# VectorE turns u by blocks of 32 in the loop's pairs, the narrow products change banks, and A's first row tile has a transfer of its own

## The chip, the cores and the metric

One NeuronCore of a Trainium2 chip runs the whole kernel. The metric is the time of one execution on the device in microseconds, lower is better. Engines are named PE or TensorE (matmul), PEld (its weight loads), DVE or VectorE, ACT or ScalarE, POOL or GpSimd, SP or SyncE (here it only issues transfers).

## The reference

An adapter layer feeds a second one, and the input is added at the end. x has 2048 tokens of width 1024, everything in fp32.

```
c   = x @ W.T + 2 * (top-2 gates of 8 experts, biased by language) applied to low-rank x @ A.T, times B
z   = c @ Wf.T + bf                      (the second layer's base)
out = x + z + 2 * softmax(c @ Wrf.T) applied to low-rank c @ Af.T, times Bm
```

The gated low-rank activations of the first layer are called u (128 wide: 8 experts of rank 16), those of the second v (32 wide: 4 experts of rank 8).

## The kernel before, in words

The kernel first folds the two dense layers into one matrix (W times the second layer's weights, with seven products in place of eight, a Strassen-Winograd scheme), then applies it to the tokens. Every fp32 product is three matmuls: each operand is rounded to a short format ("high", by ScalarE) and the rest is taken by a subtraction ("low", by VectorE); the matmuls are high*high, high*low, low*high.

**Preparation** (about the first 106 us). 28 steps, `split_step(n)` on VectorE and `round_step(n)` on ScalarE, prepare a chunk of two blocks in a ring of six; TensorE multiplies it. `make_s1_t1` to `make_t4` on VectorE make the sums of blocks that later steps read, one instruction for each of four chunks (`HALF = 4`). The parts arrive by transfers that SP issues in a row. The very first chunk of A comes in two transfers, columns 256 to 511 (the row tiles 0 and 1, `row_tile(0)` and `row_tile(1)`) and then 0 to 255; its part of B comes on ScalarE's queue. TensorE keeps busy on constants (7 matmuls) until the first operands are there.

**The pairs** (16 tiles of 128 tokens, two at a time: 8 pairs). Pair 0 and pair 1 are written out (`first`, `second`), pairs 2 to 7 are "steady" and form a loop; on VectorE and ScalarE the last pair stands behind the loop, on TensorE it does not. For a pair, TensorE has in this order:

- seven narrow products (244 columns, 12 matmuls each) for gates and tails, in the order 1, 6, 2, 7, 5, 4, 3, in the banks `BANK_NA`, `BANK_NB`, `BANK_NC`; `narrow_products(j)` begins with a wait until the tails of the pair before are read (`tails_out`), since BANK_NA and BANK_NB are 4 and 5, and the tails lie in 4 and 5 (`BANK_T`);
- wide products 1, 6 and 2 (354 columns, 12 matmuls each), then `turn_u`, two 128x128 transposes of u into PSUM (L1508);
- wide product 7, `small_y` (u times the second layer's small columns: it waits for `ut_low_ready`), `lora(BANK_A)`, product 5, `lora(BANK_D)`, product 4, `mixed_tails` (waits for `vt_ready`), `lora(BANK_B)`, three `mixed`, product 3, `lora(BANK_C)`, `mixed(BANK_C)`.

VectorE adds the wide products into `rows` and the narrow ones into `narrow`, computes the gates and u (L1112 to L1145), adds u2 (L1153), splits the turned u into `ut_low` (L1160) after ScalarE made `ut_high` (L709), then does the softmax of the second layer, makes v and turns it with four block transposes (L1213), and splits the next pair's x (`split_x`) and block sums (`split_s`, made by `next_s`). The order of every engine is written out by hand; engines meet by semaphores that count up once a pair.

SP runs `load_pair(j + 2)`, which waits for `x_split` of each tile before it loads into the same buffer `stage`, and then `store(j)`, which waits for the adds into `rows`.

Of the kernel before, what the change touches and what calls it, by code (L numbers as in the profile page):

```python
# [5 lines left out]
def adaln_ffn_kernel(nc, part_2, part_1, part_3, part_4, tokens, gate_proj, mix_rows, language, out):  # L6
# [20 lines left out]
    P = 128  # L27
# [3 lines left out]
    HALF = KC // 2  # L31
# [51 lines left out]
    BANK_NA, BANK_NB, BANK_NC = 4, 5, 6  # L83
# [6 lines left out]
    with ctx:  # L90
# [138 lines left out]
        here_2_first = [sem(f"here_2_first_{i}") for i in range(3)]  # L229
# [95 lines left out]
        u_turned = sem("u_turned")  # L325
        ut_high_ready = sem("ut_high_ready")
# [192 lines left out]
        def scalar_program(act):  # L519
# [11 lines left out]
            copy(a_high[:, 0, 2 * P:ROWS_A], a12[:, 0, 2 * P:ROWS_A]).then_inc(first_high, 1)  # L531
# [143 lines left out]
            def pair(j, first=False, second=False, last=False):  # L675
# [37 lines left out]
                if steady and not last:  # L713
                    act.wait_ge(p2_done, j + 1)
                    round_x(j + 1, 0)
# [46 lines left out]
        def vector_program(dve):  # L762
# [8 lines left out]
            def minus(dst, a, b):  # L771
# [5 lines left out]
            low_part(a_low[:, 0, 2 * P:ROWS_A], a12[:, 0, 2 * P:ROWS_A], a_high[:, 0, 2 * P:ROWS_A])\  # L777
                .then_inc(first_low, 1)
            dve.wait_ge(first_b_high, 1)
            low_part(b_low[:, 0, 0:CUT[1]], b21[:, 0, 0:CUT[1]], b_high[:, 0, 0:CUT[1]]).then_inc(first_low, 1)  # L780
            dve.wait_ge(first_high, 2)
            low_part(a_low[:, 0, 0:2 * P], a12[:, 0, 0:2 * P], a_high[:, 0, 0:2 * P]).then_inc(first_low, 1)
            dve.wait_ge(first_high, 3)
            low_part(b_low[:, 0, CUT[1]:HB], b21[:, 0, CUT[1]:HB], b_high[:, 0, CUT[1]:HB]).then_inc(first_low, 1)
            dve.wait_ge(first_high, 4)
# [30 lines left out]
            def make_s4(k):  # L816
                dve.wait_ge(f_s2, k + 1)
                minus(s4[:, k, :], a12[:, k, :], s2[:, k, :]).then_inc(f_s4, 1)

            def make_t2(k):  # L820

                dve.wait_ge(here_4[k], 16)
                dve.wait_ge(f_t1, k + 1)
                minus(t2[:, k, :], b22[:, k, :], t1[:, k, :]).then_inc(f_t2, 1)

            def make_s3(k):

                dve.wait_ge(f_s1, k + 1)
                minus(s3[:, k, :], a11[:, k, :], a21[:, k, :]).then_inc(f_s3, 1)

            def make_t3(k):

                dve.wait_ge(here_4[k], 16)
                dve.wait_ge(f_t1, k + 1)
                minus(t3[:, k, :], b22[:, k, :], b12[:, k, :]).then_inc(f_t3, 1)

            def make_t4(k):
                dve.wait_ge(f_t2, k + 1)
                minus(t4[:, k, :], b21[:, k, :], t2[:, k, :]).then_inc(f_t4, 1)
# [87 lines left out]
            for k in range(1, HALF):  # L927
                make_s4(k)
# [11 lines left out]
            make_t2(2)  # L940
            make_t2(3)
            split_step(13)
            for k in range(HALF):
                make_s3(k)
# [17 lines left out]
            for k in range(HALF):  # L962
                make_t3(k)
# [15 lines left out]
            for k in range(HALF):  # L979
                make_t4(k)  # L980
# [70 lines left out]

            def pair(j, first=False, second=False, last=False):
                steady = not first and not second
                base = STEPS * j + VEC_START
# [93 lines left out]

                if not first:
                    dve.wait_ge(stored[0], 16 * j)  # L1150
                dve.wait_ge(r1_read, j + 1)
                dve.wait_ge(p6_done, j + 1)
                add_sums(rows[:, 0, wide_at(1)], bank(BANK_B), rows[:, 1, wide_at(0)]).then_inc(u2_read, 1)  # L1153
# [5 lines left out]
                dve.wait_ge(ut_high_ready, j + 1)  # L1159
                low_part(ut_low[:, :, :], ut_psum, ut_high[:, :, :]).then_inc(ut_low_ready, 1)  # L1160
                if first:
                    split_t(T4, C11)
                if second:
                    split_tn(T2)

                    make_tn(C11, C21, C11, t4n_made)
                    next_s(S1)
                    next_s(S2)
                    next_s(S3)

# [13 lines left out]
                if steady:  # L1184
                    add_u3()
# [10 lines left out]
                if second:  # L1196
                    next_s(S4)
# [18 lines left out]
                if steady:  # L1216
                    add_r22()
# [13 lines left out]
                if steady and not last:  # L1231
                    split_s(j + 1, S3)

# [17 lines left out]
                add_sums(rows[:, 1, wide_at(0)], bank(BANK_B), rows[:, 1, wide_at(0)]).then_inc(b_out, 1)  # L1251
                if not last:
# [14 lines left out]
        def tensor_program(pe):  # L1267
# [46 lines left out]
            for dt in range(2):  # L1314
                rows_product(0, dt, 0, HH)
# [321 lines left out]
```

## Time and profile before

| | |
|---|---|
| median of 3 runs | 324.57 us (324.01 to 324.74) |
| profiled execution | 324.45 us |
| its span, first to last instruction | 323.1 us |
| PE busy | 319.5 us, 99% of the span |
| DVE busy | 245.1 us, 76% |
| ACT busy | 127.9 us, 40% |
| transfers | 27.55 MB, mean 85 GB/s |
| granted TensorE clock | 1.000 |

The 1.35 us between the span and the execution's time lie before the first and behind the last instruction. Busy time is a sum over the span; a timeline gives for each instruction its start, its duration and, in brackets, how long its engine had stood idle and for whom. Consecutive instructions of an engine overlap a little in such rows, so the distance between two starts is what one costs.

### The profile page before, as it was taken

Reading aid. Unit: us, or ns where it says so; the run is one execution under the profiler, and the core shown is the slowest. Engines: PE = TensorE matmul, PEld = TensorE weight load, DVE = VectorE, ACT = ScalarE, POOL = GpSimd, SP = SyncE. Lnnn points to the kernel's source line nnn. Section 1 sums busy time; section 2 is a strip of 40 time slices with the busy share of each in tenths; the row PEclk is TensorE's granted clock in tenths of the full one; section 3 lists DMA queues with packets and bytes.
Section 4 is the critical chain, followed back from the end, with each engine's and each line's share of the span. In section 5 each row is a group of like instructions: output and inputs, shape, how many; then the busy total and the mean of one; then the engine's idle time right before and its main releaser. Section 6 shows DMA issues by size and latency. Waiting matters only on the chain.

```text
span 323.1 us, 5951 instructions
## 1 busy us (share of the span) xinstructions
PE 319.5 (99%) x2255; PEld 313.4 (97%) x2255; DVE 245.1 (76%) x540; ACT 127.9 (40%) x253; POOL 1.4 (0%) x11
## 2 busy tenths in 40 slices
PE   8999999999999999999999999999999999999996
PEld 5999999999999899899999999999999999999996
DVE  3999999998799778988866856757585595665543
ACT  3882846495147236225413503411430340342111
POOL 1000000000000000000000000000000000000000
PEclk9999999999999999999999999999999999999999
DMA  7999000000000311700330250060042015003003
GB/s 261 416 408 284 9 2 0 2 0 2 0 2 0 132 30 40 262 0 0 115 149 0 73 187 0 14 245 0 0 144 116 0 65 195 0 0 130 0 0 130
DMA packets 10702, 27.55 MB, mean 85 GB/s; under 512 B 3166, under 2 KB 4702, under 8 KB 10688
## 3 DMA queue, kind: packets, MB, share of 16 engines
q1 hardware_dynamic: 10256, 26.83, 23.5%
q10 hardware_dynamic: 432, 0.53, 0.5%
q8 instruction: 9, 0.15, 0.2%
q14 instruction: 5, 0.04, 0.0%
HBM read 18.97 MB, written 8.39 MB: 85 GB/s over the span
## 4 chain that ended last, share of the span: by engine, by line
PE 98%; DMA 1%; DVE 0%; issue 0%
PE sums L1269 97%; DMA in<-part 1%; PE sums L1508 1%; DVE rows L1047 0%; DVE b_high L775 0%
## 5 line engine op out<-in xcount | busy, mean ns | idle before, releaser
L1269 PE MATMUL sums<-b_high,a_high 128*128 128x256 f32 (+1 forms) x224 | 45.9, 289 | 0.2 <-DVE b_high L775 0.2
L1269 PE MATMUL sums<-b_low,a_high 128*128 128x256 f32 (+1 forms) x224 | 45.5, 287 | 0.0
L1269 PE MATMUL sums<-b_high,a_low 128*128 128x256 f32 (+1 forms) x224 | 45.5, 286 | 0.0
L1269 PEld LDWEIGHTS sums<-b_high,a_high 128*128 128x128 f32 x224 | 35.2, 191 | 1.1 <-ACT a_high L527 1.1
L1269 PEld LDWEIGHTS sums<-b_low,a_high 128*128 128x128 f32 x224 | 35.1, 191 | 0.0
L1269 PEld LDWEIGHTS sums<-b_high,a_low 128*128 128x128 f32 x224 | 34.9, 190 | 0.0
L1047 DVE TENSOR_TENSOR rows<-sums,rows 128x354 f32<-128x354 f32 x48 | 24.4, 522 | 9.7 <-PE sums L1269 9.3
L1047 DVE TENSOR_TENSOR narrow<-sums,narrow 128x244 f32<-128x244 f32 x30 | 12.4, 412 | 25.6 <-PE sums L1269 25.6
L1269 PE MATMUL sums<-t_high,s_high 128*128 128x354 f32 x96 | 31.6, 329 | 0.0
L1269 PE MATMUL sums<-t_low,s_high 128*128 128x354 f32 x96 | 31.1, 324 | 0.0
L1269 PE MATMUL sums<-t_high,s_low 128*128 128x354 f32 x96 | 31.1, 324 | 0.0
L1269 PE MATMUL sums<-ct_high,st_high 128*128 128x244 f32 (+1 forms) x80 | 25.6, 320 | 0.0
L1269 PE MATMUL sums<-ct_low,st_high 128*128 128x244 f32 (+1 forms) x80 | 25.5, 319 | 0.0
L1269 PE MATMUL sums<-ct_high,st_low 128*128 128x244 f32 (+1 forms) x80 | 25.5, 319 | 0.0
L693 ACT ACTIVATE pair_exp<-top 128x1 f32<-128x1 f32 x16 | 3.9, 287 | 48.1 <-DVE top_at L1120 48.0
L527 ACT ACTIVATE s_high<-s_plain 128x512 fp32r<-128x512 f32 x28 | 17.3, 626 | 13.1 <-PE sums L1269 12.4
L1269 PE MATMUL sums<-c_high,st_high 128*128 128x354 f32 x64 | 21.0, 328 | 0.0
L1269 PE MATMUL sums<-c_low,st_high 128*128 128x354 f32 x64 | 20.8, 325 | 0.0
L1269 PE MATMUL sums<-c_high,st_low 128*128 128x354 f32 x64 | 20.7, 324 | 0.0
L769 DVE TENSOR_TENSOR b_low<-in,b_high 128x530 fp32r<-128x530 f32 (+2 forms) x29 | 19.9, 687 | 0.0
L769 DVE TENSOR_TENSOR s_low<-s_plain,s_high 128x512 fp32r<-128x512 f32 x28 | 18.9, 685 | 0.0
L1269 PEld LDWEIGHTS sums<-t_low,s_high 128*128 128x128 f32 x96 | 18.2, 189 | 0.0
(149 smaller groups left out, 821.9 us busy)
## 6 DMA issues: line engine op xcount, KB each, us to landing
stage<-tokens SPq DMA_DIRECT2D x14, 512.0 KB, 4.1
out<-rows SPq DMA_DIRECT2D x14, 512.0 KB, 4.8
in<-part SPq DMA_DIRECT2D x7, 585.0 KB, 9.0
in<-part SPq DMA_DIRECT2D x4, 777.0 KB, 14.1
in<-part SPq DMA_DIRECT2D x4, 265.0 KB, 16.6
rows<-tokens SPq DMA_DIRECT2D x2, 512.0 KB, 14.1
out<-rows SPq DMA_DIRECT2D x3, 192.0 KB, 2.3
c_plain<-gate_proj SPq DMA_DIRECT2D x1, 544.0 KB, 18.3
```

Of the source, the lines that this page charges most:

```text
L527: return nc.scalar.activation(out_, in_, ACT.Copy)
L693: ins = nc.scalar.activation(pair_exp[:, t:t + 1], top[:, t, 0:1], ACT.Exp, bias=top[:, t, 1:2], scale=-1.0)
L769: return nc.vector.tensor_tensor(dst, src, as_f32(high), ALU.subtract)
L1047: return nc.vector.tensor_tensor(dst, n, onto, ALU.add)
L1269: return nc.tensor.matmul(out_, lhs, rhs, start=start, stop=stop, skip_group_check=True)
L1508: last = nc.tensor.transpose(ut_psum[:, t, :], u[:, t, :], ident[:, :])
```

## The change

Four things, of which the first is the largest.

1. **u is turned by VectorE in pairs 2 to 6.** 16 transposes of 32-row blocks write into the gate columns of `narrow`, which are free once u is made. After the first 8 a semaphore lets ScalarE round the first half, after 16 the second; VectorE splits each half. The turned u no longer goes through PSUM. TensorE's last pair stands behind the loop (`last=True`) and keeps its own transposes, as do pairs 0 and 1.
2. **TensorE's order in pairs 2 to 6.** Product 5 goes ahead of `small_y`; `lora(BANK_B)` and product 3 go ahead of `mixed_tails`. VectorE and ScalarE follow: the adds of u3 and r22 come right after the split of u, `next_s(S4)` behind the maximum of the second softmax, the splits of S2 and S3 later, ScalarE's rounding of x's first tile before that of u.
3. **Banks.** The narrow products use 6, 7 and 4 in place of 4, 5 and 6; the wait for `tails_out` moves from before narrow product 1 to before narrow product 5, and ScalarE waits for `tails_out` before its first narrow copy.
4. **The start.** A's row tiles 0 and 1 come in two transfers and are rounded, split and multiplied in two pieces. The sums S3, T3, T4 are made in one instruction each in place of four, S4 in two, T2 in three.

```diff
-    BANK_NA, BANK_NB, BANK_NC = 4, 5, 6
+    BANK_NA, BANK_NB, BANK_NC = 6, 7, 4
...
+        def ut_plain_at(partitions, c, n):
+            h, c = divmod(c, P // 2)
+            return narrow[partitions, :, h, c:c + n]
+        def ut_plain_half(h):
+            return narrow[:, :, h, 0:P // 2]
+        def half_of(t, h):
+            return t[:, :, h * P // 2:(h + 1) * P // 2]
...
-            sp.dma_start(in_2[:, 0, 2 * P:ROWS_A], part_2[0, :, 2 * P:ROWS_A]).then_inc(here_2_first[0], 16)
+            sp.dma_start(in_2[:, 0, row_tile(0)], part_2[0, :, row_tile(0)]).then_inc(here_2_first[0], 16)
+            sp.dma_start(in_2[:, 0, row_tile(1)], part_2[0, :, row_tile(1)]).then_inc(here_2_first[3], 16)
...
                 if steady:
+                    act.wait_ge(tails_out, j)
                     act.wait_ge(p1n_done, j - 1)
...
+                if steady and not last:
+                    act.wait_ge(p2_done, j + 1)
+                    round_x(j + 1, 0)
+                if steady and not last:
+                    act.wait_ge(u_half_turned, j - 1)
+                    copy(half_of(ut_high, 0), ut_plain_half(0)).then_inc(ut_half_high, 1)
                 act.wait_ge(u_turned, j + 1)
-                copy(ut_high[:, :, :], ut_psum).then_inc(ut_high_ready, 1)
+                if steady and not last:
+                    copy(half_of(ut_high, 1), ut_plain_half(1)).then_inc(ut_high_ready, 1)
+                else:
+                    copy(ut_high[:, :, :], ut_psum).then_inc(ut_high_ready, 1)
...
-            for k in range(HALF):
-                make_s3(k)
+            make_s3()
...
+            def turn_u(j):
+                dve.wait_ge(u_ready, j + 1)
+                for h in range(2):
+                    for q in range(h * P // BLOCK // 2, (h + 1) * P // BLOCK // 2):
+                        rows_at = slice(q * BLOCK, (q + 1) * BLOCK)
+                        for i in range(P // BLOCK):
+                            at = slice(i * BLOCK, (i + 1) * BLOCK)
+                            ins = nc.vector.transpose(ut_plain_at(at, q * BLOCK, BLOCK), u[rows_at, :, at])
+                    ins.then_inc((u_half_turned, u_turned)[h], 1)
...
-                if steady:
-                    next_s(S4)
-                    if not last:
-                        split_s(j + 1, S2)
+                if turning:
+                    turn_u(j)
+                    dve.wait_ge(ut_half_high, j - 1)
+                    low_part(half_of(ut_low, 0), ut_plain_half(0), half_of(ut_high, 0))
                 dve.wait_ge(ut_high_ready, j + 1)
+                if turning:
+                    low_part(half_of(ut_low, 1), ut_plain_half(1), half_of(ut_high, 1)).then_inc(ut_low_ready, 1)
...
+                if turning:
+                    add_u3()
+                    add_r22()
...
+                if turning:
+                    split_s(j + 1, S2)
...
+                if turning:
+                    split_s(j + 1, S3)
                 if not last:
                     split_x(j + 1, 1)
...
             def narrow_products(j):
-                pe.wait_ge(tails_out, j)
...
+                pe.wait_ge(tails_out, j)
                 pe.wait_ge(s_split, 4 * j + S_NO[S1])
                 narrow_of_s(BANK_NC, S1, tn_high[T1], tn_low[T1], True).then_inc(p5n_done, 1)
...
-                if steady:
+                if last:
                     turn_u()
...
                 of_s(BANK_B, S3, t_high[T3], t_low[T3], False).then_inc(p7_done, 1)
+                if turning:
+                    product_5(j)
                 if steady:
                     small_y()
                 lora(BANK_A, 0, 0)
...
+                if turning:
+                    lora(BANK_B, 1, 0)
+                    product_3(j)
+                    mixed_tails(j)
...
-            with pe_loop(2, PAIRS) as j:
+            with pe_loop(2, PAIRS - 1) as j:
                 pair(j)
+            pair(PAIRS - 1, last=True)
```

## Rows read from the trace of the kernel before

**Rows 1.** Waits of TensorE: line, releaser: total us, times, longest.
```profile
PE sums L1269 <- PEq L1630: 0.8, 1, 0.8
PE sums L1269 <- DVE b_high L775: 0.2, 1, 0.2
```
**Rows 2.** The chain that ended last (start, us), then busy time in one pair.
```profile
226.67 0.22 PE sums L1508 x2
226.89 27.10 PE sums L1269 x192
...
211.10:238.40 27.30, 27.30 (x196) 27.28 (x195) 18.39 (x51) 8.18 (x20) 0.00 (x0) 1.00 0.22 77
```
**Rows 3.** Timeline of VectorE and ScalarE in pair 4: start, duration.
```profile
225.08 0.52 DVE L1047 TENSOR_TENSOR rows<-sums,rows 128x354 f32<-128x354 f32 x1
...
227.21 1.05 ACT L527 ACTIVATE st_high<-stage 128x1024 fp32r<-128x1024 f32 x1
...
231.88 0.97 DVE L1213 STREAM_TRANSPOSE vt_plain<-v 32x64 f32<-32x64 f32 x4
...
233.77 0.41 DVE L769 TENSOR_TENSOR vt<-vt_plain,vt 32x256 fp32r<-32x256 f32 x1 [0.35 <-ACT vt L527]
```
**Rows 4.** Timeline of TensorE, starts of turn_u, small_y, mixed_tails, narrow products 7 and 3.
```profile
226.51 0.38 PE L1508 MATMUL sums<-ident,u 128*128 128x128 f32 x2
...
228.68 0.32 PE L1269 MATMUL sums<-c_high,ut_high 128*128 128x352 f32 x1
...
234.55 0.46 PE L1269 MATMUL sums<-mix,vt 98*128 98x316 f32 x2
...
242.51 0.39 PE L1269 MATMUL sums<-t_narrow,s_high 128*128 128x244 f32 x2
...
246.62 0.27 PE L1269 MATMUL sums<-ct_high,s_high 128*128 128x244 f32 x1
```
**Rows 5.** Timeline of VectorE behind mixed_tails and into pair 5.
```profile
235.36 0.68 DVE L769 TENSOR_TENSOR s_low<-s_plain,s_high 128x512 fp32r<-128x512 f32 x1
235.96 0.81 DVE L1047 TENSOR_TENSOR rows<-sums,narrow 128x632 f32<-128x632 f32 x1
236.69 0.95 DVE L1047 TENSOR_TENSOR rows<-sums,rows 128x354 f32<-128x354 f32 x2
237.55 1.21 DVE L769 TENSOR_TENSOR st_low<-stage,st_high 128x1024 fp32r<-128x1024 f32 x1
238.69 0.52 DVE L1047 TENSOR_TENSOR rows<-sums,rows 128x354 f32<-128x354 f32 x1
239.15 0.69 DVE L769 TENSOR_TENSOR s_low<-s_plain,s_high 128x512 fp32r<-128x512 f32 x1
241.43 0.41 DVE L1047 TENSOR_TENSOR narrow<-sums,narrow 128x244 f32<-128x244 f32 x1 [1.58 <-PE sums L1269]
...
244.41 0.68 DVE L877 TENSOR_TENSOR s_plain<-stage 128x512 f32<-128x512 f32 x1
```
**Rows 6.** Loads of x into stage, 225 to 262 us: issues (start of first and last), landing.
```profile
L451 SPq DMA_DIRECT2D stage<-tokens x2: 354/354/355, 235.7 to 238.9; - x2
...
DMA to landing us min/median/max: 3.5/3.7/4.0
```
**Rows 7.** Timeline of the start; last, window 3 to 4 us, DMA share before the GB/s.
```profile
3.72 0.29 DVE L775 CAST b_high<-in 128x256 fp32r<-128x256 f32 x1 [1.92 <-DMA in<-part]
...
4.13 0.50 PEld L1269 LDWEIGHTS sums<-b_high,a_high 128*128 128x128 f32 x2 [1.10 <-ACT a_high L527]
...
4.92 0.29 ACT L527 ACTIVATE bt_high<-in 128x128 fp32r<-128x128 f32 x1
...
7.83 0.64 ACT L527 ACTIVATE a_high<-in 128x512 fp32r<-128x512 f32 x1 [2.62 <-DMA in<-part]
...
8.76 1.16 PE L1269 MATMUL sums<-b_high,a_high 128*128 128x256 f32 x8
...
3.00:4.00 1.00, 0.93 (x3) 0.03 (x1) 0.28 (x2) 0.42 (x1) 0.00 (x0) 1.00 1.10 393
```
**Rows 8.** DMA queues of the page: packets, MB, share of 16 engines' span.
```profile
q8 instruction: 9, 0.15, 0.2%
```

More of the change, by code:

```diff
@@ L228, in adaln_ffn_kernel @@
         here_4 = [sem(f"here_4_{k}") for k in range(HALF)]
-        here_2_first = [sem(f"here_2_first_{i}") for i in range(3)]
+        here_2_first = [sem(f"here_2_first_{i}") for i in range(4)]
         gate_here = sem("gate_here")
@@ L814, in make_s2, with make_s4, make_t2, make_s3 @@
                 minus(s2[:, k, :], s1[:, k, :], a11[:, k, :]).then_inc(f_s2, 1)
[L816 to L839, printed above, removed]
+            def make_s4(k, n=1):
+                dve.wait_ge(f_s2, k + n)
+                minus(s4[:, k:k + n, :], a12[:, k:k + n, :], s2[:, k:k + n, :]).then_inc(f_s4, n)
+            def make_t2(k, n=1):
+                for i in range(k, k + n):
+                    dve.wait_ge(here_4[i], 16)
+                dve.wait_ge(f_t1, k + n)
+                minus(t2[:, k:k + n, :], b22[:, k:k + n, :], t1[:, k:k + n, :]).then_inc(f_t2, n)
+            def make_s3():
+                dve.wait_ge(f_s1, HALF)
+                minus(s3, a11, a21).then_inc(f_s3, HALF)
+            def make_t3():
+                dve.wait_ge(f_t1, HALF)
+                minus(t3, b22, b12).then_inc(f_t3, HALF)
+            def make_t4():
+                dve.wait_ge(f_t2, HALF)
+                minus(t4, b21, t2).then_inc(f_t4, HALF)
             def add_out(q, c, lower, onto):
@@ L926, in vector_program @@
             make_s2(3)
-            for k in range(1, HALF):
-                make_s4(k)
+            make_s4(1, 3)
             make_t2(0)
@@ L961, in vector_program @@
             split_step(15)
-            for k in range(HALF):
-                make_t3(k)
+            make_t3()
             dve.wait_ge(lang_here, 16)
@@ L978, in vector_program @@
             split_step(16)
-            for k in range(HALF):
-                make_t4(k)
+            make_t4()
             for n in range(17, 20):
@@ L1050, in vector_program @@
             BLOCK = 32
+            def turn_u(j):
[7 more added lines that the diff above has]
+                    ins.then_inc((u_half_turned, u_turned)[h], 1)
             def pair(j, first=False, second=False, last=False):
                 steady = not first and not second
+                turning = steady and not last
                 base = STEPS * j + VEC_START
@@ L1195, in pair @@
                                         negate=True).then_inc(neg_max_ready, 1)
-                if second:
+                if second or turning:
                     next_s(S4)
@@ L1313, in tensor_program @@
             pe.wait_ge(first_b_high, 1)
-            for dt in range(2):
-                rows_product(0, dt, 0, HH)
+            rows_product(0, 0, 0, HH)
             pe.wait_ge(first_low, 1)
-            for dt in range(2):
-                rows_product(0, dt, 0, LH)
+            rows_product(0, 0, 0, LH)
+            pe.wait_ge(first_high, 2)
+            rows_product(0, 1, 0, HH)
             pe.wait_ge(first_low, 2)
@@ L1463, in narrow_products, with product_3, pair @@
                 narrow_of_s(BANK_NC, S4, cn_high[B22], cn_low[B22], False).then_inc(p3n_done, 1)
-            def pair(j, first=False, second=False):
+            def product_3(j):
+                pe.wait_ge(s_split, 4 * j + 4)
+                pe.wait_ge(r22_read, j + 1)
+                of_s(BANK_C, S4, cw_high[B22], cw_low[B22], False).then_inc(p3_done, 1)
+            def pair(j, first=False, second=False, last=False):
                 steady = not first and not second
+                turning = steady and not last
                 s_no = S_NO_FIRST if first else S_NO
@@ L1523, in pair @@
                 of_x(BANK_A, 0, 1, cw_high[B21], cw_low[B21], False).then_inc(p2_done, 1)
-                if steady:
+                if last:
                     turn_u()
-                else:
+                if not steady:
                     small_y()
@@ L1536, in pair @@
                 lora(BANK_A, 0, 0)
+                if second or last:
+                    product_5(j)
                 if not first:
-                    product_5(j)
                     pe.wait_ge(d_out, j)
@@ L1545, in pair @@
                 of_x(BANK_B, 1, 1, t_high[T4], t_low[T4], False).then_inc(p4_done, 1)
-                if not steady:
+                if turning:
+                    lora(BANK_B, 1, 0)
+                    product_3(j)
+                    mixed_tails(j)
+                elif last:
+                    mixed_tails(j)
+                    lora(BANK_B, 1, 0)
+                else:
                     lora(BANK_B, 1, 0)
                     mixed_tails(j)
-                else:
-                    mixed_tails(j)
-                    lora(BANK_B, 1, 0)
                 mixed(BANK_A, 0, 0).then_inc(a_done, 1)
```

65 lines of the change are left out of this document (33 added, 32 removed).

## The prediction

> **What bounds the kernel now.** I read four views, in this order. The first is the list of waits, to see whether TensorE ever stands still: it waits twice, 0.8 us for its sequencer and 0.2 us for VectorE's first rounding, both before 4.2 us [rows 1]. The second is the chain that ended last, to see what fills the rest: it is TensorE alone, in the loop 27.10 us of matmuls and 0.22 us for the two transposes of u, pair after pair [rows 2]. So the kernel is one stream of matmuls. Work taken out of that stream is time won, work taken off any other engine is worth nothing, and any wait put into the stream costs its whole length. The third view is the timeline of one pair by engine, for how early each semaphore comes before TensorE asks for it. The fourth is the first 10 us, where the stream depends on transfers.
>
> **What leaves the stream.** In the pairs 2 to 6 TensorE no longer transposes u: 5 x 0.22 = 1.1 us less [rows 2]. Pair 7 keeps its transposes. All other matmuls stay, in another order. At this size a page of the Trainium skill can be weighed. The row says 0.22 us for two fp32 transposes. The page "VectorE: DVE Perf Modes", section "The three transpose paths", gives 390 ns for one 128x128 transpose on TensorE (bf16); by it 5 x 2 x 0.39 = 3.9 us would go, an estimate from that page, and the time would be 320.6. The trace has a duration for this very operation, so the row decides.
>
> **What VectorE gets.** 16 block transposes a pair, each of 32x64 elements, the shape it already turns v in: four of those take 0.97 us at 0.232 us each, so one begins 0.246 us after the other [rows 3]. Sixteen take 15 x 0.246 + 0.232 = 3.92 us. Their partitions differ from v's (the output moves over four groups of 32, with v the input does), and no row shows that form. Bounds: from below 0.14 us apart, if they overlapped by the 0.09 us that other VectorE instructions do (0.52 us long and 0.43 apart) [rows 5]; from above 0.30 apart, if each were as long as a 128x128 instruction on ScalarE, 0.29 [rows 7]. I take 0.246, the same shape. VectorE is not the bound: it works 18.4 us in the 27.3 of a pair [rows 2], so there is room for the sum; what matters is two places where its result is due.
>
> *Place one, before small_y.* Times in the clock of rows 3 to 6, with the change written into that pair. The add of u2 starts at 225.08 as now [rows 3], the transposes at 225.52, their end is 229.44. The first half is rounded and split under the second. ScalarE's rounding of x, 1.05 us [rows 3], now stands ahead of it but begins when product 2 is done, near 226.8, and ends before 227.9. The second half: ScalarE 229.48 to 229.77 (0.29), VectorE to 230.08 (0.29, from the same bound). TensorE reaches small_y at 228.68 [rows 4] - 0.22 + 1.95 for product 5, now ahead of it (product 7 is as long: 228.68 - 226.51 - 0.22) = 230.41. At the start the first weight load comes 0.12 us after VectorE's end (4.01 to 4.13) [rows 7], and a load takes 0.11 of its own, since two transposes with a load each pass in 0.22; so the semaphore is due at 230.41 - 0.23 = 230.18. **It is 0.10 early.** Cost 0; if that cover is gone each 0.1 us is 0.5 us in all.
>
> *Place two, before narrow product 7 of the next pair.* Product 3 and lora(BANK_B) now stand before mixed_tails, which starts at 234.55 - 0.22 + 0.49 + 1.95 = 236.77 [rows 4], 2.22 us later. Behind it VectorE has the tails add (0.73 to the next start), two adds (0.86), the split of S3 that was moved here (0.60), the split of x's second tile (1.14), the add of c (0.46), the split of S1 (0.60), the narrow u2 add (0.41) [rows 5]: 4.80 us from 237.26, so 242.06. Narrow product 7 starts at 242.51 - 0.22 = 242.29 [rows 4], so its semaphore is due at 242.06. **It is exactly in time**: 0 to 0.1 us a pair. I take 0, and keep 5 x 0.1 = 0.5 us for the range.
>
> **Other edits of the loop.** vt is ready at 234.18 for mixed_tails at 234.55 [rows 3, 4]. Its chain begins with small_y, 1.73 us later, and mixed_tails is 2.22 later: more room than now. The new banks let narrow products 1, 6, 2 and 7 start before the tails are read; TensorE doesn't wait there today [rows 1], so nothing is won. ScalarE's and TensorE's moved waits on the tails end at 238.07 (237.26 + 0.81), when narrow product 1 still runs: it is three products of 1.37 us before product 7 [rows 4] and ends at 239.55. SP is moved too: the load of x's second tile waits for the split of x, now done at 240.66 instead of 238.76. It lands 3.5 to 4.0 us after its issue, some 0.14 us behind the split [rows 6], at 244.3 to 244.8, and the sum S1 that is due at 244.41 - 0.22 = 244.19 [rows 5] waits 0.1 to 0.6 us. The add queued behind it, r22n, is needed for narrow product 3 at 246.62 - 0.22 [rows 4]; at the latest it starts 0.61 behind S1, at 245.4, and with 0.41 is done at 245.8, due at 246.17, 0.35 us early. The stores, queued behind that load on SP, wait for the add of c, over at 241.1; the next add of u2, which waits for them, is at 225.08 + 27.1 = 252.2, 11 us later, and a load of the same 512 KB takes 4.0 at most. Cost 0.
>
> **The start.** Now A's first tile is 64 KB in its own transfer, and every later transfer on SP is issued some 0.45 us later. The first weight load, at 4.13, follows the rounding of b (3.72 to 4.01) [rows 7], which is not A's, so A's half size brings little. Whatever it brings ends at the next chunk: its a is rounded from 7.83 to 8.47, and the matmuls that read it start at 8.76 without a gap [rows 7], due 0.23 earlier at 8.53. A gain is capped at 0.06 us. A loss: if issue set the landings, chunk 1 lands 0.45 late and costs 0.4. But from 3 us on the DMA engines are full (share 1.10) [rows 7], so their rate sets it and the late issue is hidden. The smaller rows make more packets; I take 0.05 lost, range -0.06 to +0.4. The merged make_s3, make_s4, make_t2, make_t3 and make_t4 do in one instruction what up to four did, 0.6 us apart [rows 5]; their first chunk comes up to 1.8 us later and their last no later. TensorE has no wait in all this stretch [rows 1], but how much room it had I leave open: 0 as long as VectorE runs three chunks ahead.
>
> **The peeled last pair.** TensorE now leaves a loop once. No row shows it leaving one. From below 0, the way straight code runs; from above one fetch of instructions: 9 packets took 0.2% of 16 engines' 323.1 us, 1.15 us each [rows 8]. I take 0, since pairs 0 and 1 run as straight code without a wait [rows 1].
>
> **Sum.** The profiled execution took 324.45 us, 323.1 of it span. 324.45 - 1.1 + 0.05 = 323.4. The median of the runs is 324.57, 0.12 above it, so 323.5.
>
> **Rivals.**
> (a) *The stream closes up, as summed*: 323.5; its own range 323.2 to 323.8. For it: both places close at measured durations. Chance 0.57.
> (b) *Waits of 0.1 to 0.2 us a pair take the transposes' place*, at narrow product 7 above all, or chunk 1 lands late at the start: 0.5 to 1.0 us given back, 324.0 to 324.5, no measurable change. For it: the margin of 0.00 and of 0.10. Against: both use start-to-start times of the same instructions. Chance 0.25.
> (c) *The slower side: the block transposes are dearer than v's.* At distance d the wait at small_y is 15 x (d - 0.246) - 0.10 a pair, five times; it eats the gain from d = 0.267 and makes the kernel slower by 0.2% from d = 0.275. At the upper bound 0.30 it is 0.7 us a pair, 3.5 in all: 327.0. Against: v's transposes too change their partitions from one to the next, and all take 0.232 us. Chance 0.10. The skill's page "VectorE: DVE Perf Modes" says in "Rules for kernel authors" that a 128x128 transpose belongs on TensorE when PSUM may take it; by that rule this rival is the one to expect. In the trace TensorE is the full engine and VectorE has a third of its time free, which speaks the other way.
> (d) *Leaving the loop costs a fetch*, once: 323.5 + 1.15 = 324.65, no change. Chance 0.08. The skill's "Runtime: NRT & Kernel Launch", section "Instruction fetch mechanics", says that a taken branch out of the fetched window stalls; the loop's branch back costs nothing in [rows 1], and the way out is not taken but fallen through.
>
> **How the numbers follow.** A measurement here tells about 0.2%, 0.65 us, from no change: faster means under 323.92, slower over 325.22. (a) is faster; of (b) a fifth is; (c) is half slower, half same; (d) is the same, with a third of it slower by a longer fetch. Faster 0.57 + 0.05 = 0.62; slower 0.05 + 0.03 = 0.08, and 0.02 more for two rivals at once, 0.10; same the rest, 0.28. The range goes from the fast end of (a), with the 0.3 us by which a median of runs moves, 322.9, to the upper end of (b), 324.6; above lie (c) and part of (d).
>
> **What would show it.** In the profile after: 10 fewer transposes of L1508's kind but 80 more block transposes; chain of the loop 27.10 us per pair with no 0.22 piece; TensorE's waits still below about 1 us in all. Right at place one: the ut_low split ends 0.1 us before small_y could start. Wrong in (b): a wait of TensorE on `narrow` (narrow product 7) or on b or a of chunk 1. Wrong in (c): mean of a block transpose over 0.25 us, a wait on ut_low five times. Wrong in (d): one wait of TensorE near 293 us that no engine releases.

## The result and the profile after

The changed kernel takes 324.84 us (median of 20 executions, 323.99 to 327.97), the kernel before beside it 324.46 (20, 323.94 to 325.24). The ratio over all executions is 1.003, interval 1.0016 to 1.0044: slower by 0.3%. The forecast was 323.5 and faster. The executions of the changed kernel lie in two groups, 12 at 323.99 to 325.0 and 8 at 325.91 to 327.97, with nothing between; the kernel before has no second group. The profiled execution, at 323.99, is the shortest of the first group. So its profile shows the milder case.

The page of the changed kernel first: span, then busy time, share and instructions of each engine.

```profile
span 322.7 us, 6000 instructions
...
PE 318.1 (99%) x2245; PEld 311.8 (97%) x2245; DVE 263.2 (82%) x614; ACT 128.5 (40%) x259; POOL 1.4 (0%) x11
```

TensorE is busy 1.4 us less than the 319.5 of before, VectorE 18.1 us more. Of the 1.4 the forecast has 1.1, the transposes taken out. The next view, the waits of TensorE, answers to [rows 1] and shows what came in (PEq and SPq are the parts of TensorE and SyncE that issue their work).

```profile
PE sums L1313 <- DVE a_low L796: 0.9, 1, 0.9
PE sums L1313 <- PEq L1690: 0.8, 1, 0.8
```

The 0.2 us for b_high is gone, and in its place stands 0.9 us for a_low. The chain that ended last says where:

```profile
1.21 0.42 SPq L445
...
1.67 3.41 DMA in<-part
...
5.11 0.42 ACT a_high L543
...
5.55 0.43 DVE a_low L796
...
6.03 110.52 PE sums L1313 x846
...
143.29 164.57 PE sums L1313 x1164
307.86 0.22 PE sums L1562 x2
```

Two things are to be read. From 143.29 on the loop is one piece of 164.57 us with no 0.22 in it: pairs 2 to 6 no longer turn u, and no listed wait stands in their place. In the kernel before the same stretch (from behind the transposes of pair 1 to those of pair 7) lasts 165.66, so the loop gained 1.09 us; the forecast was 1.1. And TensorE's unbroken stream now begins at 6.03, behind a transfer, where it began at 4.13 [rows 7]. The timeline of the start, same columns as [rows 7]:

```profile
1.67 0.43 SPq L446 DMA_DIRECT2D in<-part  x1
...
3.12 0.31 ACT L543 ACTIVATE a_high<-in 128x128 fp32r<-128x128 f32 x1 [0.15 <-DMA in<-part]
3.32 0.29 DVE L802 CAST b_high<-in 128x256 fp32r<-128x256 f32 x1 [1.52 <-DMA in<-part]
...
3.76 0.51 PE L1313 MATMUL sums<-b_high,a_high 128*128 128x256 f32 x1
...
4.06 0.31 ACT L543 ACTIVATE a_high<-in 128x128 fp32r<-128x128 f32 x1 [0.63 <-DMA in<-part]
...
5.11 0.42 ACT L543 ACTIVATE a_high<-in 128x256 fp32r<-128x256 f32 x1 [0.73 <-DMA in<-part]
...
5.55 0.42 DVE L796 TENSOR_TENSOR a_low<-in,a_high 128x256 fp32r<-128x256 f32 x1 [0.86 <-ACT a_high L543]
...
6.03 0.50 PE L1313 MATMUL sums<-b_high,a_high 128*128 128x256 f32 x2 [0.87 <-DVE a_low L796]
...
8.08 0.63 ACT L543 ACTIVATE a_high<-in 128x512 fp32r<-128x512 f32 x1 [2.04 <-DMA in<-part]
```

The first matmul on real data comes earlier, at 3.76. But the transfer of A's columns 0 to 255 (L446) is now third on SP's queue. It goes out at 1.67, and its rounding starts at 5.11. TensorE is through with row tiles 0 and 1 at about 5.2 and stands until 6.03. Chunk 1 is late too, 8.08 against 7.83 [rows 7], but here TensorE doesn't wait for it: its matmuls start at 9.10, 0.34 us after the 8.76 of before, and that distance is already 0.36 at 6.37 (6.01 before). In this execution the first of pair 0's transposes comes at 116.56 instead of 116.22, a loss of 0.34 us. The rest of the 0.9 was won before and just behind the wait: 0.40 by the earlier beginning (3.76 for 4.16), since B's first part is rounded at 3.32 instead of 3.72 [rows 7], and 0.13 because the matmuls reach their full rate earlier. In the kernel before, two matmuls of 256 columns still took 0.43 us at 5.58; here two take 0.23 at 4.65.

The windows of the start, with DMA share and GB/s as the last two columns, answer to the last of [rows 7]:

```profile
3.00:4.00 1.00, 1.00 (x4) 0.30 (x3) 0.68 (x3) 0.31 (x1) 0.00 (x0) 1.00 0.92 287
4.00:5.00 1.00, 0.96 (x6) 0.72 (x6) 0.44 (x2) 0.31 (x1) 0.00 (x0) 1.00 0.93 255
```

The DMA engines show a busy share of 0.92 between 3 and 4 us where it was 1.10, and move 287 GB/s where they moved 393: the rate fell by more than the share.

The loop, pair 4, at the two places that the forecast watched:

```profile
225.48 3.99 DVE L1083 STREAM_TRANSPOSE narrow<-u 32x64 f32<-32x64 f32 x16
229.50 0.64 DVE L796 TENSOR_TENSOR ut_low<-narrow,ut_high 128x128 fp32r<-128x128 f32 x2
...
230.38 0.33 PE L1313 MATMUL sums<-c_high,ut_high 128*128 128x352 f32 x1
...
241.59 0.41 DVE L1070 TENSOR_TENSOR narrow<-sums,narrow 128x244 f32<-128x244 f32 x1
...
242.25 0.39 PE L1313 MATMUL sums<-t_narrow,s_high 128*128 128x244 f32 x2
...
245.16 0.69 DVE L905 TENSOR_TENSOR s_plain<-stage 128x512 f32<-128x512 f32 x1 [0.93 <-DMA stage<-tokens]
```

Sixteen block transposes take 3.99 us, 0.25 from start to start (3.92 forecast). ut_low is done at 230.14 (230.08), small_y starts at 230.38 (230.41). The narrow u2 add ends at 242.00 (242.06), narrow product 7 starts at 242.25 (242.29). TensorE waits at neither. The late load of x's second tile makes VectorE wait 0.93 us here, and next to nothing of it reaches TensorE. One pair earlier the wait is 1.04 us, and there some of it does, at the first matmul of narrow product 3 (`ct_high,s_high`):

```profile
218.08 0.69 DVE L905 TENSOR_TENSOR s_plain<-stage 128x512 f32<-128x512 f32 x1 [1.04 <-DMA stage<-tokens]
...
219.06 0.27 PE L1313 MATMUL sums<-t_narrow,st_low 128*128 128x244 f32 x1
219.24 0.35 PE L1313 MATMUL sums<-ct_high,s_high 128*128 128x244 f32 x1
219.43 0.27 PE L1313 MATMUL sums<-ct_low,s_high 128*128 128x244 f32 x1
```

The distances are 0.18 and 0.19 us where such matmuls otherwise start 0.11 apart, 0.15 us lost. The list of waits doesn't have it, since these rows overlap by 0.16 us (0.27 long, 0.11 apart) and a shorter delay leaves no gap.

### The profile page after: what moved, and what is told of

It reads as the page before. It is cut to its first block, busy times and chain, and to the rows that moved or that the text cites. A ratio compares the mean times of both kernels' runs of the same rounds, so it can differ in the third digit from the quotient of the medians.

```text
span 322.7 us, 6000 instructions
## 1 busy us (share of the span) xinstructions
PE 318.1 (99%) x2245; PEld 311.8 (97%) x2245; DVE 263.2 (82%) x614; ACT 128.5 (40%) x259; POOL 1.4 (0%) x11
## 4 chain that ended last, share of the span: by engine, by line
PE 97%; DMA 1%; DVE 0%; SPq 0%; ACT 0%; issue 0%
PE sums L1313 97%; DMA in<-part 1%; PE sums L1562 0%; DVE rows L1070 0%; DVE a_low L796 0%; ACT a_high L543 0%; SPq L445 0%; SPq L444 0%
## 5 line engine op out<-in xcount | busy, mean ns | idle before, releaser
L1083 DVE STREAM_TRANSPOSE narrow<-u 32x64 f32<-32x64 f32 x80 | 18.8, 235 | 1.1
```

The costliest lines, as they stand in the source:

```text
L1083: ins = nc.vector.transpose(ut_plain_at(at, q * BLOCK, BLOCK), u[rows_at, :, at])
```

## Experiments

Each kernel was timed beside the kernel before on the same chip: 324.23, 324.34 and 324.37 us in the three groups. "New loop" is everything of the change but the start.

### Which half costs: the whole again, the new loop alone, the new start alone

`e4_after_again` is the changed kernel once more.

> The changed kernel itself again, for its spread beside the other three on one chip and for a second profile. Both theories: ratio 1.002 to 1.005, executions from 324.0 to 328. Theory S: if the profiled execution is a slow one, its loop is again 27.09 us a pair and all of the loss lies before 12 us. Theory L: the loop's pairs are unequal.

`e1_old_start` puts back the start and keeps the rest:

```diff
-            sp.dma_start(in_2[:, 0, row_tile(0)], part_2[0, :, row_tile(0)]).then_inc(here_2_first[0], 16)
-            sp.dma_start(in_2[:, 0, row_tile(1)], part_2[0, :, row_tile(1)]).then_inc(here_2_first[3], 16)
+            sp.dma_start(in_2[:, 0, 2 * P:ROWS_A], part_2[0, :, 2 * P:ROWS_A]).then_inc(here_2_first[0], 16)
...
-            copy(a_high[:, 0, row_tile(0)], a12[:, 0, row_tile(0)]).then_inc(first_high, 1)
-            act.wait_ge(here_2_first[3], 16)
-            copy(a_high[:, 0, row_tile(1)], a12[:, 0, row_tile(1)]).then_inc(first_high, 1)
+            copy(a_high[:, 0, 2 * P:ROWS_A], a12[:, 0, 2 * P:ROWS_A]).then_inc(first_high, 1)
...
```

The splits on VectorE and the order of the first matmuls go back with it.

> The changed kernel with its start put back (A's row tiles 0 and 1 in one transfer, rounded, split and multiplied together as before); loop, banks and merged sums stay changed. Theory S (the start is what went wrong: in the profile after, A's columns 0 to 255 came third on SP's queue, TensorE waited 0.87 us for them at 5.1 us, and in some executions the clock falls as well): the time is 1.1 us below the kernel before, 323.4, ratio 0.996 to 0.998, mean clock 0.998 or more in nearly all executions, all within 1.5 us. Theory L (the slow executions come from the loop, where x's second load now lands at the time it is read): executions still spread over 3 to 4 us, a third of them above 325.8, ratio 1.000 to 1.003.

`e2_new_start_alone` is the kernel before with only that part of the diff put in, the other way round.

> The kernel before with the new start alone (two transfers for A's row tiles 0 and 1, two roundings, two splits, the new order of the first matmuls); loop, banks and sums as before. Theory S: 0.4 us later than before in a good execution (324.9), and in a third of the executions 1.5 to 3 us later, part of them with a mean clock of 0.993 to 0.995; ratio 1.003 to 1.006. Theory L: 0.4 us later throughout, ratio about 1.001, no execution above 325.8.

| | median us (range) | ratio to before |
|---|---|---|
| e4, all | 326.09 (324.64 to 326.65) | 1.0044 (1.0028 to 1.006) |
| e1, new loop | 323.36 (323.06 to 324.11) | 0.9968 (0.9956 to 0.998) |
| e2, new start | 326.41 (324.93 to 328.29) | 1.006 (1.0036 to 1.0085) |

The new loop gains 0.3% (0.87 us by the medians, 1.04 by the ratio), the new start costs 0.6%. e4 falls into the two groups again, 4 executions at 324.64 to 324.95 and 8 at 325.94 to 326.65. Its profiled execution, at 325.96, is one of the upper group, and its waits and windows show what happened in it. Columns of the windows as in [rows 7]: PE busy with its matmuls (x) first, and the granted clock before the DMA share.

```profile
PE sums L1313 <- DVE a_low L796: 1.4, 1, 1.4
...
7.00:8.00 1.00, 1.00 (x6) 1.00 (x6) 0.00 (x0) 0.00 (x0) 0.00 (x0) 0.50 1.05 351
8.00:9.00 1.00, 1.00 (x7) 1.00 (x6) 0.24 (x1) 0.24 (x1) 0.00 (x0) 0.50 0.94 365
9.00:10.00 1.00, 1.00 (x6) 1.00 (x6) 0.96 (x3) 0.59 (x2) 0.00 (x0) 0.50 1.00 407
```

TensorE waits 1.4 us until 6.47, and just behind that the granted clock is 0.50, the lower of its two levels (1.2 GHz), for three us: 6 or 7 matmuls in each instead of 10 or 11. Against the profiled execution of the first time the span is 1.9 us longer (324.6 to 322.7): the unbroken stream begins 0.44 us later (6.47 for 6.03), and its first piece, the same 846 matmuls, takes 112.06 us instead of 110.52, 1.54 by the clock. The loop's piece is 164.49 against 164.57, so nothing of this is lost in the loop. The window from 7 us on has 10 matmuls in e1:

```profile
7.00:8.00 1.00, 1.00 (x10) 1.00 (x9) 0.29 (x1) 0.29 (x1) 0.00 (x0) 1.00 0.93 356
```

The Trainium skill's page "TensorE: Matmul & The Clock Gate", section "What's actually happening", says that the lower clock is the default and that activity of the array releases the higher one. The rows agree: the fall of the clock stands behind the one long wait.

### The transfers or the pieces

The start changed two things, two transfers for one and two pieces of work for one. `e5_one_transfer_pieces` is the changed kernel with one transfer, the pieces kept:

```diff
-            sp.dma_start(in_2[:, 0, row_tile(0)], part_2[0, :, row_tile(0)]).then_inc(here_2_first[0], 16)
-            sp.dma_start(in_2[:, 0, row_tile(1)], part_2[0, :, row_tile(1)]).then_inc(here_2_first[3], 16)
+            sp.dma_start(in_2[:, 0, 2 * P:ROWS_A], part_2[0, :, 2 * P:ROWS_A]).then_inc(here_2_first[0], 16)
...
-            act.wait_ge(here_2_first[3], 16)
```

> The changed kernel with A's row tiles 0 and 1 again in one transfer of 128 KB; they are still rounded, split and multiplied in two pieces. Theory T (the additional transfer ahead of A's columns 0 to 255 and of every chunk on SP's queue is the whole loss): no wait of TensorE over 0.4 us before 10 us, ratio 0.996 to 0.998, as the kernel with the old start (0.9968). Theory P (the two pieces and their new order on VectorE and TensorE cost too): ratio above 0.999.

`e6_two_transfers_whole` is e1 with the two transfers of the change (their lines aren't shown), and one rounding behind both:

```diff
             act.wait_ge(here_2_first[0], 16)
+            act.wait_ge(here_2_first[3], 16)
             copy(a_high[:, 0, 2 * P:ROWS_A], a12[:, 0, 2 * P:ROWS_A]).then_inc(first_high, 1)
```

> The old start with the additional transfer alone: row tiles 0 and 1 come in two transfers, ScalarE waits for both and rounds them together; matmuls in the old order. Theory T: columns 0 to 255 land 0.9 us late, TensorE waits about 0.6 to 1.2 us for their split, ratio 1.002 to 1.007, a third or more of the executions above 325.6. Theory P: ratio 0.997 to 0.999, no execution above 325.

e5 measured 323.57 (323.31 to 323.91), ratio 0.9975 (0.9967 to 0.9984), in one group: the pieces cost nothing that can be told (e1 has 0.9968). e6 measured 326.21 (325.68 to 327.08), 1.0057 (1.0044 to 1.0069), 5 executions, but its trace shows a second cause, so that it decides nothing. Timeline of ScalarE, then a window:

```profile
3.98 1.28 ACT L543 ACT_TABLE_LOAD   x1 [3.98 <-DMA in<-part]
5.28 0.72 ACT L543 ACTIVATE a_high<-in 128x256 fp32r<-128x256 f32 x2
...
6.00:7.00 1.00, 1.00 (x5) 1.00 (x6) 1.00 (x4) 0.53 (x3) 0.00 (x0) 1.00 0.91 370
```

With two waits ahead of the first rounding, the load of ScalarE's table stood behind the first of them: 3.98 instead of 1.69. TensorE began at 5.75, behind a wait of 1.8 us, at 5 to 7 matmuls in a us until 11.9. The column of the clock says 1.00 there, because the trace has no record of the clock before 11.91 us; in the trace of the kernel before the first is at 6.04, where the matmuls become faster. So a low clock at the very start shows in the count of matmuls and not in that column. This could explain why 4 of the 8 long executions of the changed kernel, and all 5 of e2's, are listed with a mean clock of 1.000; none of them was profiled, so it isn't shown. `e9_two_transfers_one_wait` repeats the question with a single wait (against e1):

```diff
-            sp.dma_start(in_2[:, 0, 2 * P:ROWS_A], part_2[0, :, 2 * P:ROWS_A]).then_inc(here_2_first[0], 16)
+            sp.dma_start(in_2[:, 0, row_tile(0)], part_2[0, :, row_tile(0)]).then_inc(here_2_first[0], 16)
+            sp.dma_start(in_2[:, 0, row_tile(1)], part_2[0, :, row_tile(1)]).then_inc(here_2_first[0], 16)
...
-            act.wait_ge(here_2_first[0], 16)
+            act.wait_ge(here_2_first[0], 32)
```

> As e6_two_transfers_whole, but both transfers raise one semaphore and ScalarE waits for it once, so that its table load isn't held behind the first wait (in e6 it began at 3.98 us in place of 1.69). Theory T (the additional transfer alone is the loss): row tile 1 lands near 4.0 us, columns 0 to 255 near 5.0, TensorE starts at 4.6 to 4.8 and waits again before the second half; ratio 1.000 to 1.005 with a group of slow executions. If e6 was slow by its table load alone: ratio 0.996 to 0.998.

It measured 325.25 (324.13 to 326.99), 1.0024 (1.001 to 1.0038), where the same program with one transfer (e1) had 0.9968. Six of its 12 executions lie at 325.65 or above, five of these with a mean clock of 0.994 or 0.995. Its profiled one, at 326.99 us, waits for both parts of A and shows the fall:

```profile
PE sums L1310 <- DVE a_low L794: 1.1, 1, 1.1
...
PE sums L1310 <- ACT a_high L543: 0.5, 1, 0.5
...
7.00:8.00 1.00, 1.00 (x7) 1.00 (x7) 0.21 (x2) 0.00 (x0) 0.00 (x0) 0.50 0.98 365
```

So it is the second transfer, not the pieces (0.9 us of that one execution is lost in the loop, as shown below). Up to 6 us the changed kernel moved this,

```profile
DMA packets 856, 1.19 MB, mean 199 GB/s; under 512 B 89, under 2 KB 729, under 8 KB 856
```

and e1, with the same bytes to fetch, this:

```profile
DMA packets 765, 1.42 MB, mean 236 GB/s; under 512 B 78, under 2 KB 590, under 8 KB 765
```

That is 91 more packets and 0.23 MB less. Both the late issue of columns 0 to 255 (1.67 for 1.21) and the smaller packets can delay them; how the two share the delay was not taken apart.

### The place in the queue, and the clock by itself

`e7_columns_on_act` leaves both transfers and exchanges what comes next: A's columns 0 to 255 go second on ScalarE's queue, the rest of B's first chunk third on SP's.

```diff
-            sp.dma_start(in_2[:, 0, 0:2 * P], part_2[0, :, 0:2 * P]).then_inc(here_2[0], 16)
+            sp.dma_start(in_2[:, 0, ROWS_A + CUT[1]:IN_W], part_2[0, :, ROWS_A + CUT[1]:IN_W])\
+                .then_inc(here_2_first[2], 16)
...
-            act.dma_start(in_2[:, 0, ROWS_A + CUT[1]:IN_W], part_2[0, :, ROWS_A + CUT[1]:IN_W])\
-                .then_inc(here_2_first[2], 16)
+            act.dma_start(in_2[:, 0, 0:2 * P], part_2[0, :, 0:2 * P]).then_inc(here_2[0], 16)
```

> The changed kernel, with A's columns 0 to 255 as the second transfer on ScalarE's queue and the rest of B's first chunk (201 KB) as the third on SP's: the two swap queues. Theory T: columns 0 to 255 are there near 4.5 us, as before the change, the rest of B is needed 0.7 us after them; TensorE waits 0 to 0.4 us, ratio 0.996 to 0.999. If it is the number of transfers or the smaller rows that cost and not the place in the queue: as the changed kernel, 1.003 or more.

`e8_constants_in_the_gap` gives TensorE five matmuls on constants in the place of the wait, as it has them before its first operands. The late transfer stays late.

```diff
+            for _ in range(5):
+                mm(bank(BANK_WARM, 0, BANK), ones[:, 0:P], ones, start=True, stop=True)
             pe.wait_ge(first_low, 4)
             tiles_product(0, 1, 0)
```

> The changed kernel, and TensorE multiplies constants five times (512 columns, 1.07 us at the upper clock) into an unused bank where it waited for A's columns 0 to 255. Theory C (the wait has a second price: TensorE's idleness of 0.9 to 1.4 us in the first microseconds makes the clock fall to its lower level for some 3 us in part of the executions, 1.5 to 2 us each): the slow group disappears, all executions within 1 us around 324.0 to 324.7, ratio 0.998 to 1.001. If the slow group is only a later landing, it stays: executions above 325.8, ratio 1.003 or more.

e7: 324.18 (323.83 to 324.7), ratio 0.9997 (0.9988 to 1.0006). The wait of 0.9 us is now two of 0.2 us, and no execution is above 324.7. The place of the transfer was most of the loss, and the upper group goes with the wait. But e7 just misses its 0.996 to 0.999, and it is still 0.6 us above e5, timed beside it with one transfer; that part stays open.

e8: 324.75 (323.92 to 325.34), 1.0014 (1.0005 to 1.0022), also just outside what was expected. The upper group is gone here too. That doesn't give the price of the late data, since the constants outlast the wait. In the profiled execution A's split is done at 5.80, and TensorE takes 1.58 us for the five, part of them still at the lower rate:

```profile
5.34 1.93 PE L1313 MATMUL sums<-const-bfloat16-1.0 128*128 128x512 bf16 x5
6.92 0.59 PE L1313 MATMUL sums<-b_high,a_high 128*128 128x256 f32 x2
```

The two parts of the price are better read from the groups. The lower group of e4 has its median at 324.73, 1.4 us above e1's 323.36 beside it. The upper groups lie higher by another 1.6 us (e4) and 1.9 us (the first timing).

What sorts an execution into a group is not shown. The profiled ones with a second transfer give a hint: TensorE had reached its full rate at about 3.5 us in the two in which the clock fell (e4, with a wait of 1.4 us; e9, with 0.5 and 1.1), by 4.4 in the changed kernel's first (0.9 us, no fall) and near 5 us in e2 (1.1 us, no fall).

### The loop: what gains, and how near the two places are

`e12_order_without_turning` is e1 in which TensorE turns u in pairs 2 to 6 as before, while orders, banks and merged sums stay new:

```diff
-                if last:
+                if steady:
                     turn_u()
...
-                if turning:
-                    turn_u(j)
-                    dve.wait_ge(ut_half_high, j - 1)
-                    low_part(half_of(ut_low, 0), ut_plain_half(0), half_of(ut_high, 0))
```

> The version with the old start, with the new order, banks and merged sums, but u is turned by TensorE into PSUM in pairs 2 to 6 as before (and ScalarE and VectorE round and split it whole). Theory G (the gain of the loop is the transposes and nothing else): 1.1 us above e1_old_start, ratio 1.000, between 0.9993 and 1.001. If order, banks or merged sums gave part of the gain: below 0.999.

It measured 324.43 (324.1 to 324.93), ratio 1.0003 (0.9995 to 1.0012), and its chain is that of [rows 2] again:

```profile
226.31 0.22 PE sums L1544 x2
226.53 27.09 PE sums L1297 x192
```

By the medians it is 1.1 us above e1 (beside another group of runs). The whole gain of the loop is the ten transposes; the new order only makes room for VectorE's, and banks and merged sums cost nothing that can be told.

`e10_two_more_turns` and `e11_two_turns_before_narrow` are e1 with two more block transposes in each turn, into a tile that nobody reads: ahead of VectorE's turning of u (pairs 2 to 6), or ahead of the narrow u2 add (pairs 2 to 7).

```diff
+                    dve.wait_ge(u_ready, j + 1)
+                    for i in range(2):
+                        nc.vector.transpose(spare[0:BLOCK, :, i * BLOCK:(i + 1) * BLOCK], u[0:BLOCK, :, i * BLOCK:(i + 1) * BLOCK])
                     turn_u(j)
```

> The version with the old start (0.9968), and in pairs 2 to 6 VectorE makes two more block transposes, into a spare tile, ahead of the sixteen: 0.49 us more before the second half of u is split. Theory M (the margin before small_y is 0.10 us, as worked out in the prediction): TensorE waits 0.4 us in each of five pairs, 1.9 us in all, ratio 1.002 to 1.004. If the margin is larger than 0.5 us: ratio 0.997 as without them.

> The version with the old start (0.9968), and in pairs 2 to 7 VectorE makes two more block transposes, into a spare tile, ahead of the narrow add of u2: 0.49 us. Theory M (the margin before narrow product 7 is 0 to 0.05 us in pairs 3 to 7): TensorE waits 0.45 us in each of five pairs, 2.2 us in all, ratio 1.003 to 1.005. If the margin is larger than 0.5 us: ratio 0.997.

e10: 324.47 (323.99 to 324.89), 1.0 (0.9992 to 1.0009). e11: 325.07 (324.87 to 325.65), 1.0021 (1.0012 to 1.003). Both lose, but less than expected (1.002 to 1.004 and 1.003 to 1.005), since the two extra transposes took less time. Timeline of VectorE and TensorE in e10:

```profile
225.20 0.35 DVE L1203 STREAM_TRANSPOSE spare<-u 32x64 f32<-32x64 f32 x2
225.48 1.19 DVE L1080 STREAM_TRANSPOSE narrow<-u 32x64 f32<-32x64 f32 x5
...
229.98 0.32 PE L1313 MATMUL sums<-t_high,s_low 128*128 128x354 f32 x1
230.16 0.43 PE L1313 MATMUL sums<-c_high,ut_high 128*128 128x352 f32 x1
230.43 0.32 PE L1313 MATMUL sums<-c_low,ut_high 128*128 128x352 f32 x1
```

Two cost 0.28, 0.14 each; both read the same 32 partitions and write the same 32. The turning of u, which writes to others each time, stays at 0.24 to 0.25 (five in 1.19), and so do the four of v, which write to the same 32 partitions but read others each time (0.246 apart [rows 3]). The Trainium skill's page "VectorE: DVE Perf Modes", section "Two Vector instructions with no wait between them", says that an instruction whose input or output starts in another group of 32 partitions than the last one's is held until the earlier have finished; these rows agree.

The loop's piece of the chain is 165.53 in e10 and 165.47 in e11, against 164.50 in e3 below. The starts of TensorE's matmuls say where the 1.0 us goes. In e10 small_y (230.16) and its second matmul start 0.18 and 0.27 us behind the one before, where 0.16 is usual: 0.13 lost, and 0.12 to 0.15 in each of the five pairs. From 0.28 added, so place one has about 0.15 us of room, 0.10 by the forecast. The other 0.3 us of e10 is lost at narrow product 3, in three pairs. In e11 narrow product 7 loses 0.22 a pair in four pairs and 0.15 in the fifth, from 0.29 added. So place two has about 0.07 us; the forecast had 0.00. By the ratios e11 is 1.7 us above e1. Some 1.0 of it is the loop; in its profiled execution 0.2 more is a wait for chunk 1, which landed at 8.06; the rest stays open.

`e3_old_start_load_early` is e1 with `split_x(j + 1, 1)` ahead of `split_s(j + 1, S3)`, so that SP issues the load of x's second tile earlier.

```diff
-                if turning:
-                    split_s(j + 1, S3)
                 if not last:
                     split_x(j + 1, 1)
+                if turning:
+                    split_s(j + 1, S3)
```

> As e1_old_start, and VectorE splits x's second tile before S3 in pairs 2 to 6, so that SP can issue the load of x 0.6 us earlier. Theory S: the same as e1_old_start, 323.4. Theory L: fewer slow executions than e1_old_start, median at least 0.3 us lower.

323.55 (323.14 to 323.81), 0.9971 (0.9961 to 0.9982): by the times the same as e1. The profiled executions differ. The loop's piece in e1 and e3, then in e9, which has e1's loop:

```profile
142.78 165.06 PE sums L1309 x1164
...
143.22 164.50 PE sums L1309 x1164
...
145.52 76.27 PE sums L1310 x540
221.79 0.11 issue
221.90 88.94 PE sums L1310 x624
```

In e3 VectorE waits for that load only in pair 1, and from one small_y to the next TensorE takes 27.09 us from pair 2 to pair 6. In e1 it waits 0.97 to 1.07 us in pairs 2 to 5, and narrow product 3 of the next pair comes 0.1 to 0.2 us late each time, 0.6 us in all. In e9 the wait reaches 1.24 us and the loss is 0.9; in e4 and e6, with waits up to 0.9 us, there is none. So in the same code the late load costs TensorE 0 to 0.9 us an execution, and it costs where VectorE waits more than about 0.9 us. e1's profiled execution is its longest (324.11), and e3's lost 0.5 us at the start, to a wait for chunk 1, so that the medians don't show what the earlier load is worth.

## Why the prediction failed

**What bounds the kernel** held. One stream of matmuls; work taken out of it was won in full, and waits put into it were paid. What did not hold is that a wait costs its length: 0.9 us cost 0.34 against the profiled execution of before, since the beginning was earlier, and 1.4 us in e4 was followed by 1.5 us of lower clock.

**What leaves the stream** held: 1.1 forecast, 1.09 in the chain, 0.87 to 1.04 in e1's times, nothing without it (e12).

**VectorE's two places** held, to 0.06 us each, with no wait of TensorE; the room measured is about 0.15 us at the first and 0.07 at the second (0.10 and 0.00 forecast). Rival (b)'s waits of 0.1 to 0.2 us a pair did not come at these places, but at narrow product 3 they came, in one pair of the changed kernel's first profile and in four of e1's. Rival (c) did not: the transposes take 0.236 us in the mean, 0.25 apart. Rival (d) did not: no wait near 293 us.

**The other edits of the loop** held for the banks, the moved waits and the merged sums. The load of x's second tile was taken for free with 0.35 us to spare before narrow product 3; it lands up to 4.3 us after its issue instead of 4.0, S1 waits 0.85 to 1.04 us in pairs 2 to 5 where 0.1 to 0.6 was forecast, and the room is used up: 0.15 us lost in that profile, 0 to 0.9 us in others. That the loop's gain still came out at 1.09 in it is partly luck, since that execution had the loss in one pair only.

**The start is the step that failed**, the term "I take 0.05 lost, range -0.06 to +0.4". It followed the first transfer (little gained, where the first matmul in fact came 0.40 us earlier, since B's first part was there earlier) and chunk 1 (0.25 us late, inside the range) and passed over the transfer between them, A's columns 0 to 255, which went from second to third on SP's queue. Its reason, "the DMA engines are full, so their rate sets it and the late issue is hidden", took a busy share for a fixed rate: the share was 0.92 and the rate 287 GB/s instead of 393. Those columns were rounded at 5.11 instead of 4.28, TensorE waited 0.9 to 1.4 us, and 8 of 20 executions took about 1.9 us more. The two long ones of that kind that were profiled (in e4 and e9) spent it on the lower clock behind the wait; for the others the clock is argued, not shown. In the term's own units: measured is 324.84 - (324.46 - 1.10) = 1.5 us by the medians of the first timing, and 326.09 - 323.36 = 2.7 by e4 and e1, where 8 of 12 executions lie in the upper group. With 1.5 in place of the sum's 0.05 the forecast would have been 325.0. No rival had this mechanism (of the start, (b) had chunk 1 alone), and the bound of 0.4 allowed for a later issue alone, neither for the rate nor for what the clock does with a pause.

## What to carry over

A transfer ahead of others delays everything behind it on its queue: list each of those with the moment at which it is needed, not only the one that is split. In a kernel whose start is fed just in time, a wait of about 1 us there can cost over 2, since the clock may fall behind it. Work on constants in a gap that can't be closed kept the upper group away, but it must not outlast the gap, as it did in e8. The loop's change is worth keeping with one transfer for A's first two row tiles: e1 (0.9968), e3 (0.9971) and e5 (0.9975) all beat both kernels. A margin that is worked out to 0.1 or 0.4 us should be read in several profiles: one trace showed almost no loss at narrow product 3, another 0.9 us.

## What the runs showed of the hardware that was not expected

- A wait of TensorE of 1.4 us (e4, until 6.47 us) or 1.1 us (e9, until 6.71) was followed by some 3 us at granted clock 0.50, while 0.9 us in another execution of e4's program and 1.1 us in e2 were not. With five matmuls on constants in the gap none of 12 executions lay in the upper group (e8).
- Where TensorE began real work only at 5.75 us, it ran at half its rate of matmuls until 11.9 us with the clock's column at 1.00 (e6). In the kernel before it did so until 6 us (6 matmuls between 5 and 6 us, 9 in the next).
- ScalarE's table load, 1.28 us, can come to stand behind a wait for data: at 3.98 us instead of 1.69 when a second wait was put ahead of the first rounding (e6), not with one wait (e9).
- Block transposes of 32x64 elements start 0.14 us apart when they read the same 32 partitions and write the same 32 (e10), and 0.25 when each writes to others (u's) or reads from others (v's).
- In the first 6 us of the changed kernel 91 more packets carried 0.23 MB less than in e1.
